# A graph network on one core: scatters spread over the dense loop, eight early groups fewer, and logits summed by ScalarE

## The reference

```
k = typed_matmul(h, k_lin, node_type)       # 4 node types
q = typed_matmul(h, q_lin, node_type)
t_edge = einsum('nd,rde->rne', q, rel_att)[etype, dst]   # 8 edge types
score  = sum(t_edge * k[src], axis=-1)      # one logit per edge
logits = score * (rel_pri / sqrt(64))[etype]
m      = segment_max(logits, dst);  ex = exp(logits - m[dst])
alpha  = ex / segment_sum(ex, dst)[dst]     # then a weighted sum of messages by dst
```

## Time and profile before

| what | value |
|---|---|
| median of 3 runs | 6645.62 us (6629.22 to 6647.14) |
| the profiled execution | 6621.41 us, its span 6619.6 us |
| mean granted TensorE clock | 0.762 of full speed |
| busy in the span | TensorE 72%, weight loads 40%, VectorE 67%, ScalarE 36%, GpSimd 56% |
| dense block | first L621 at 169.0 us, last at 1672.7 us |
| scores block | first gather at 1713.5 us, last at 2719.2 us |

### The profile page before, as it was taken

How to read it: one execution, slowest core, us unless ns; L and a number is a source line. 1 busy time by engine, 2 the same in 40 slices (tenths; PEclk the granted TensorE clock), 3 DMA queues, 4 the chain that set the end, 5 groups by cost and what they waited for, 6 DMA issues and landing times. The chain is left out here.

```text
span 6619.6 us, 72686 instructions
## 1 busy us (share of the span) xinstructions
PE 4767.0 (72%) x18455; PEld 2642.0 (40%) x18455; DVE 4454.2 (67%) x7915; ACT 2385.6 (36%) x6652; POOL 3727.8 (56%) x3983
## 2 busy tenths in 40 slices
PE   0101477766799999789997888566587878778886
PEld 0100255544444455356664444222233334444443
DVE  5100488866788888699996666566567766666666
ACT  0100388756433333245553333122122333333333
POOL 1777300155466666200007887888777757777787
PEclk9655799988899999899995555555578877776666
DMA  9000133344333344299993332344455542222221
GB/s 353 21 7 14 56 117 118 116 122 125 85 84 84 84 85 88 52 264 286 285 268 84 83 83 75 98 112 112 95 145 148 150 112 64 64 64 65 64 60 41
DMA packets 845867, 733.47 MB, mean 111 GB/s; under 512 B 545388, under 2 KB 552514, under 8 KB 845328
## 3 DMA queue, kind: packets, MB, share of 16 engines
q1 hardware_dynamic: 543408, 519.54, 27.2%
q0 software_dynamic: 102464, 90.84, 7.5%
q10 hardware_dynamic: 199584, 118.45, 5.9%
HBM read 455.90 MB, written 276.55 MB: 111 GB/s over the span
## 5 line engine op out<-in xcount | busy, mean ns | idle before, releaser
L1366 POOL DMA_INDIRECT df_hs<-u,keep_idx x396 | 508.2, 1283 | 830.7 <-POOLq L243 710.3
L883 POOL DMA_INDIRECT sc_xg<-t,keep_gather x396 | 447.5, 1130 | 383.9 <-DVE sc_h L196 207.9
L805 POOL DMA_INDIRECT den_xd<-t,keep_gather x224 | 234.0, 1045 | 719.1 <-DMA xd<-den_xd 651.7
L1366 POOL DMA_INDIRECT hd_gat<-u,keep_idx x396 | 484.2, 1223 | 157.8 <-issue 117.4
L1899 POOL DMA_INDIRECT out_x<-hd_x,keep_scat_out x396 | 457.5, 1155 | 148.5 <-issue 119.9
L797 POOL DMA_INDIRECT t<-keep_ptr_pay,keep_scat_ptr x396 | 396.2, 1001 | 256.5 <-issue 131.9
L1366 POOL DMA_INDIRECT ml_gat<-u,keep_idx x396 | 401.8, 1015 | 157.7 <-issue 65.2
L1366 POOL DMA_INDIRECT pr_gat<-sd,keep_idxsd x396 | 413.5, 1044 | 104.3 <-issue 71.5
L220 DVE TENSOR_REDUCE den_dn_ss<-den_dn_sq 128x8 f32<-128x512 f32 x297 | 198.2, 668 | 328.9 <-issue 172.0
L754 PE MATMUL den_ps_dhid<-den_dh2t,keep_weights 64*128 64x512 f32 x396 | 129.5, 735 | 358.0 <-issue 323.9
L1355 PE MATMUL at_ps_m<-at_vx,keep_msg_twice 128*128 128x512 f32 x792 | 364.7, 604 | 23.2 <-DVE at_vx L1246 23.2
(11 more groups left out here) (314 smaller groups left out, 13003.4 us busy)
## 6 DMA issues: line engine op xcount, KB each, us to landing
u<-den_dh SPq DMA_DIRECT2D x198, 256.0 KB
t<-tab_row ACTq DMA_DIRECT2D x99, 272.0 KB, 11.3
tab_x<-in_x SPq DMA_DIRECT2D x99, 256.0 KB
den_dx<-in_x SPq DMA_DIRECT2D x99, 256.0 KB
out_x<-den_dx SPq DMA_DIRECT2D x99, 256.0 KB
sc_et<-in_etype_row SPq DMA_DIRECT2D x99, 256.0 KB
at_v<-vt SPq DMA_DIRECT2D x198, 128.0 KB
at_et<-in_etype_row SPq DMA_DIRECT2D x99, 256.0 KB
```

The source lines that it names most:

```text
L805: pool.indirect_dma_start(xd[i][:, u, :], None, e.T0, bass.IndirectOffsetOnAxis(ap=e.gather0[:, b, TU + u:TU + u + 1], axis=0), bounds_che ...
L883: pool.indirect_dma_start(xg[i][:, u, :], None, e.T0, bass.IndirectOffsetOnAxis(ap=e.gather0[:, b.n, u:u + 1], axis=0), bounds_check=NP - ...
L1366: pool.indirect_dma_start(gat[i][:, u, :], None, table, bass.IndirectOffsetOnAxis(ap=idx_all[:, c:c + 1], axis=0), bounds_check=rows - 1, ...
```

## The change

```diff
-EARLY = 56
+EARLY = 48
 LATE = [b for b in range(NG) if b * (NG - EARLY) // NG != (b + 1) * (NG - EARLY) // NG]
...
-        head = count * 66 // 99
+        head = count * 71 // 99
...
+                PACE = 6
                 for c in range(CH):
+                    if c % PACE == 0:
+                        wait(pool, den.x2_done, c // PACE, e.pool_passed)
                     pool.indirect_dma_start(pairs, bass.IndirectOffsetOnAxis(ap=e.scat_ptr[:, c:c + 1], axis=0),
...
+        lsum = s.sb("lsum", [P, TU, D])
...
-        ps_q, ps_kv, ps_r, ps_l = s.ps("q", [P, GE]), s.ps("kv", [P, GE]), s.ps("r", [D, GE]), s.ps("l", [P, TU])
+        ps_q, ps_kv, ps_r, ps_l = s.ps("q", [P, GE]), s.ps("kv", [P, GE]), s.ps("r", [D, GE]), s.ps("l", [P, TU, D])
...
                         a.wait_ge(l_ready, g.n + 1)
-                        a.copy(lmajor[:, bass.ds(g.n * TU, TU)], ps_l[:, :]).then_inc(l_kept, 1)
+                        wait(a, l_kept, g.n)
+                        for u in range(TU):
+                            c = g.n * TU + u
+                            m = a.activation(lsum[:, u, :], ps_l[:, u, :], ACT.Copy, accum_out=lmajor[:, c:c + 1])
+                        m.then_inc(l_kept, 1)
...
                         for u in range(TU):
-                            m = pe.matmul(ps_l[:, u:u + 1], prod[:, u * P:(u + 1) * P], e.C["ones"][0:D, 0:1],
-                                          start=(u == 0), stop=(u == TU - 1), skip_group_check=True)
+                            m = pe.transpose(ps_l[:, u, :], prod[:, u * P:(u + 1) * P], e.C["ident"][0:D, 0:D])
                         m.then_inc(l_ready, 1)
```

## The result

The changed kernel takes 6118.21 us (median of 4 runs, 6107.57 to 6133.83), the kernel before, run beside it, 6640.85 us (median of 4, 6629.22 to 6647.14). The ratio is 0.9217, with a 95% interval of 0.9188 to 0.9246. The profiled execution took 6107.96 us, 6106.2 of them span, 513.4 us less span than before. Mean granted clock 0.783 (0.762 before).

What follows compares the result with a forecast made beforehand. TensorE, slowed by unbroken indirect DMAs in the dense block, was taken as the bound. 6621 - 454 (dense) + 8 (moved gathers) - 27 (logits) = 6148, plus 24 for the median, 6172, rounded 6170 us; range 6075 to 6360.

Steps and rivals of the forecast that it cites:

- the first rival: Dense block: pacing frees the loop wholly, scatter price 0, 60 us more gain, 6110 us; chance 0.18.
- TensorE, held up by the stream of indirect DMAs, bounds the first stretch.: Dense block, first stretch: indirect DMAs streaming without rest slow TensorE, 66 us a step against 9.09, losing 511 us.
- The paced step: Dense block, 66 steps of six scatters: 0.15 us a scatter, 10.0 us a step, 660 us in all.
- Two signs of the prediction: Dense scatter stretch: L621 starts less than 12 us apart; L646 and L693 wait for TensorE one or two us at most.
- The 24 gathers and the rest: Dense block after the scatters: five steps with 24 gathers 58 us, then 27 steps at 12.3 us, 332 us.
- Scores: Scores block: logits summed by ScalarE instead of TensorE matmuls, gain 0.28 x 98 = 27 us.
- X: Scores block: period of one step, 9.85 us forecast against 10.13 before; bounds 9.50 and 10.3.
- The 32 moved gathers: Eight groups moved from the dense to the scores block: cost 8 us, between 0 and 16.
- The gather's price: Dense block: a paced scatter costs as a late gather, 0.51 us, 12.2 us a step, about 6315 us; chance 0.13.
- Slow recovery: Dense block: TensorE needs 25 us after each batch of six, 34 us a step, 7300 us; chance 0.04.
- The same price wherever: Dense block: a scatter costs 1.22 us wherever it stands, 16.4 us a step, about 6595 us; chance 0.04.
- The case that the stall isn't the scatters': Dense block: the loop's first steps stay at 66 us for a cause of their own, 6625 us; chance 0.04.

Runs made afterwards that it cites:

- the last experiment: The kernel before with new logits and the square root ahead of the sums, scatters unpaced: 6721.14 us against 6691.38, ratio 1.0054.

## Why the prediction was right

The time lies 52 us under the forecast of 6170, 12 us below the forecast's own span (6130 to 6240) and well inside the range. Forty of them are terms of the sum; the rest is that the median now lies 10 us above the profiled execution, not 24. The time itself is nearer to the first rival's 6110 than to the forecast; it is the step by step account that speaks for the forecast.

*TensorE, held up by the stream of indirect DMAs, bounds the first stretch.* Right for the chip that the trace came from. The reading, from a consumer's start and not from the matmul's modelled end, was the one that led there. Under the stall were the kernel before and the change at first, the last experiment, and the kernel before beside that. The other eleven experiments, on three chips, do not show it.

*The paced step.* Predicted 10.0 us, measured 638.9 / 66 = 9.68, which puts a scatter at (638.9 - 600) / 396 = 0.10 us, where 600 = 66 x 9.09. Taken was 0.15, between 0 and 0.51. Most steps are free (8.9 us), and fifteen of the 66 take 10.3 to 17.4 us; the five of over 12 us, among them the one read above and the two at the start, lie where batches met without a rest. What lengthens the other ten (10.3 to 11.1 us) wasn't read. Two signs of the prediction didn't hold everywhere: those five steps take over 12 us, and L646 and L693 wait up to 8.5 and 10.7 us, not one or two. The term as a whole gave 21 us more than forecast.

*The 24 gathers and the rest.* 58.2 us predicted at 58, 327.3 predicted at 332. SP did not wait for a gather.

*Scores.* X was put together from four terms. The root stood at 4.31 us from the transposes, not 4.6, because four sums from PSUM take 0.80 us and not the 1.10 that the row of attend gave; the masks' chain was 7.51 and not 7.69. By the prediction's own formula the step is (4.31 + 7.51 + 0.1 + 7.32) / 2 = 9.62 us, and 9.62 to 9.63 is the median step of every experiment with this order and no stall (9.70 in the change's trace). The q product does start 0.15 us behind the last mask, as named. So the mechanism was right and the delay too large: 9.62 against the 9.54 of TensorE's own work is 0.08 us, where 0.35 was taken. The block gained 35 us where 27 - 8 = 19 was forecast.

*The 32 moved gathers.* Forecast 8 us. Without the stall they cost nothing (9.684 and 9.698 us a step). Under it the mean lies 0.33 us above the median before and after alike, so no cost shows there either, though 13 steps of the change take over 10.1 us.

*The rivals.* Freed wholly (6110) came nearest: the late steps keep it out, 639 - 600 = 39 us over 66 steps. The gather's price, 0.51 us, holds in the third stretch, still 12.1 us a step, and not for batches of six. Slow recovery after each batch is out: behind the rest of 8.5 us the next steps take 9.5 and 8.9 us. The same price wherever is out by the same numbers.

The case that the stall isn't the scatters' is out on the chip of the forecast. Behind it stood the Trainium skill (SBUF — State Buffer, SBUF: two separate sides), by which a transfer and engine work do not slow each other. That fits three of the chips here: 71 to 74 us for nine steps beside an unbroken stream. It does not fit the two traces with 593 and 594 us, nor that of the change, where thirteen scatters in a row put ScalarE 5 us behind. What the forecast lacked altogether was that it held only where its trace was taken: it gave no chance to a world in which the whole 454 us is not there. Run again on another chip the same change is worth 0.74%, and all of that is the logits, the term that was the small one. The number came out because the result was measured under the same stall as the trace; where the change ran again it takes 5850 us, below the range.

## What to carry to other kernels

Read a matmul's lateness at its consumer, and when it is far larger than the work, look at which other engine streams without a rest. A loop and a stream beside it can be tied by one wait on the loop's counter, at a grain that leaves the stream a rest in each step; here that costs nothing that shows where there is no stall, and gives 472 us where there is one (66 steps in 639 us in place of 1111). Before a gain is put down to a mechanism for good, run kernel and change on a second chip: an edit that removes a contention is worth what that chip has of it, while one that removes work (0.98 us of TensorE for 0.39) was worth 38 to 53 us on each chip without the stall, and not to be counted on under it.

## What the runs showed of the hardware

*One program, two times.* The kernel before took 5883 to 5896 us on three chips, 6691 on a fourth and 6641 in the first result, whose chip isn't on record (medians), each spread within 0.7%. Each chip was seen in one condition only, within a quarter of an hour, so whether it belongs to the chip or to a state that a chip is in for a time isn't shown. The granted clock can't account for it: in the scatters it is at its lower level for most of the time (0.55 in the mean), which is half of the full one, while a step takes 112 us in place of 8.9. Later blocks are longer too. The mlp block, which no edit touches, in the change on the first chip and in the kernel with the old logits on another:

```profile
4235.00:4890.00 655.00, 509.41 (x1980) 234.54 (x1980) 443.68 (x892) 183.01 (x396) 489.66 (x792) 0.78 0.54 139
```
```profile
4077.00:4664.00 587.00, 457.47 (x1980) 208.02 (x1980) 446.78 (x892) 177.36 (x396) 486.23 (x792) 0.90 0.61 155
```

The same 1980 matmul instructions and 792 instructions of GpSimd (396 gathers and 396 small fills) stand in 655 and in 587 us. GpSimd is busy with them through the whole of it, 75% and 83% of the time. The granted clock is lower as well (0.78 and 0.90), so how much of the 68 us is the stall was not told apart.

*The stall has a size.* In the unpaced stream of both traces four steps in a row take 111 to 112 us, with 40 matmul instructions each, which is 2.8 us an instruction. The consumers in the kernel before say the same, read on from the end of the earlier trace rows:

```profile
278.06 0.58 ACT L702 COPY den_dh3t<-den_ps_dt 128x512 f32<-128x512 f32 x1 [10.09 <-remote]
283.67 0.69 ACT L709 ACTIVATE den_dhid<-den_ps_dhid,keep_weights 128x512 f32<-128x512 f32 x1 [4.49 <-issue]
289.26 0.69 ACT L709 ACTIVATE den_dhid<-den_ps_dhid,keep_weights 128x512 f32<-128x512 f32 x1 [4.91 <-remote]
```

L693 (266.86) and L702 (278.06) are four transposes apart and start 11.20 us apart; each L709 needs two matmul instructions more and comes 5.6 us later. So TensorE's results come at an even 2.8 us an instruction, whichever it is. Without the stall, in the trace with the new logits alone, L693 and L702 start at 208.47 and 209.66.

The stall outlasts the stream. The last gather is issued by 730.2 us, in the eighth step; the ninth starts behind it, at 737.7 us, and still takes 25 us, since ScalarE gets its next product of TensorE at 755.54, 25 us behind the last gather. The tenth takes 9.1.

*What stays open.* Through what an indirect DMA holds TensorE up, why on some chips alone, whether scatters without a target or fills would do it too, whether pacing the gathers recovers the 3 us a step of the last stretch (32 x 3 = 96 us at most), and why the new logits lost their gain in the last experiment. Kernels for the scatters and the gathers ran, but on chips that don't show the stall.
